# Moving the preparation of seven inputs of gated attention into the MLP, with a tile buffer of their own and a copy in DRAM

## What is computed

```
x = x + attention(layernorm(x)) @ w_ao + b_ao
x = x + attention(q from layernorm(x), k and v from ctx) @ w_co + b_co
x = x + gelu(layernorm(x) @ w1 + b1) @ w2 + b2
a = layernorm(ctx, ln_gamma, ln_beta)              # the second layer; a depends on inputs alone
Q, K, V = x @ Wq.T, a @ Wk.T, a @ Wv.T
x = x + tanh(gate) * (softmax(Q K.T / sqrt(32), masked) @ V) @ Wo.T
```

## Time and profile before

| what | value |
|---|---|
| median of 3 executions | 1102.28 us (1100.7 to 1104.54) |
| the profiled execution, its span | 1100.7 us |
| PE busy, PE weight loads busy | 1074.7 us (98%), 934.2 us (85%) |
| DVE, ACT, POOL busy | 815.4 us (74%), 712.7 us (65%), 462.0 us (42%) |
| granted TensorE clock | 1.00 throughout (2.4 GHz) |

### The profile page before, as it was taken

One profiled execution on the slowest core, in us unless ns is written; L12 is line 12 of the kernel. 1 busy time (PEld: TensorE's weight loads), 2 busy tenths in 40 slices (PEclk: granted clock), 3 DMA queues, 4 the chain that ended last, 5 costly groups with the idle time before them and its releaser, 6 DMA issues.

```text
span 1100.7 us, 24328 instructions
## 1 busy us (share of the span) xinstructions
PE 1074.7 (98%) x8829; PEld 934.2 (85%) x8829; DVE 815.4 (74%) x1314; ACT 712.7 (65%) x2365; POOL 462.0 (42%) x337
## 2 busy tenths in 40 slices
PE   7989999999999999998999999999999999999998
PEld 6888888888888888886898888888888988888886
DVE  6678787778888778888877557656677478778777
ACT  4678777777788778786444434434444387777776
POOL 3665666557767776767512121103012331122100
PEclk9999999999999999999999999999999999999999
DMA  6366565576776777553241130220622146666633
GB/s 216 98 201 198 191 195 188 174 227 216 221 227 215 223 211 229 180 191 128 85 134 40 38 96 12 85 96 1 181 101 83 59 146 205 203 198 210 177 97 97
DMA packets 136135, 167.04 MB, mean 152 GB/s; under 512 B 16992, under 2 KB 82256, under 8 KB 136016
## 3 DMA queue, kind: packets, MB, share of 16 engines
q1 hardware_dynamic: 136016, 165.50, 47.9%
HBM read 113.15 MB, written 52.29 MB: 150 GB/s over the span
## 4 chain that ended last, share of the span: by engine, by line
PE 59%; DVE 12%; ACT 9%; POOL 7%; issue 4%; DMA 3%; SPq 1%; DVEq 0%; ACTq 0%; POOLq 0%
PE psum L938 15%; PE psum L919 14%; PE psum L758 13%; POOL prob L2023 6%; PE psum L858 5%; PE psum L750 5%; ACT prob L1217 4%; ACT prob_blocks L1217 2%; PE psum L794 2%; PE psum L776 2%; DVE prob L1590 2%; DVE ln_tile L1528 2%; PE psum L835 2%; DVE negmax L1603 2%; ACT inputs_transposed L1255 2%
## 5 line engine op out<-in xcount | busy, mean ns | idle before, releaser
L758 PE MATMUL psum<-inputs_hi,weights_hi 128*128 128x256 f32 x768 | 223.7, 291 | 5.4 <-POOL inputs_lo L2014 2.5
L758 PE MATMUL psum<-inputs_lo,weights_hi 128*128 128x256 f32 x768 | 217.1, 283 | 0.0
L758 PE MATMUL psum<-inputs_hi,weights_lo 128*128 128x256 f32 x768 | 217.0, 283 | 0.0
L2014 POOL TENSOR_TENSOR inputs_lo<-inputs_transposed,inputs_hi 128x512 fp32r<-128x512 f32 x84 | 113.0, 1367 | 228.9 <-DVE inputs_hi L1563 168.4
L2023 POOL TENSOR_TENSOR prob<-prob,mask_bias 128x1024 f32<-128x1024 f32 x64 | 152.7, 2408 | 98.3 <-DVE prob L1590 96.3
L1217 ACT ACTIVATE prob<-prob,negmax 128x128 f32<-128x128 f32 x472 | 182.2, 391 | 0.5 <-DVE negmax L1603 0.5
L758 PEld LDWEIGHTS psum<-inputs_hi,weights_hi 128*128 128x128 f32 x768 | 146.7, 191 | 10.3 <-issue 2.8
L1603 DVE TENSOR_REDUCE negmax<-prob 128x8 f32<-128x1024 f32 x96 | 115.9, 1210 | 50.0 <-POOL prob L2023 50.0
L758 PEld LDWEIGHTS psum<-inputs_lo,weights_hi 128*128 128x128 f32 x768 | 147.0, 191 | 0.2
L758 PEld LDWEIGHTS psum<-inputs_hi,weights_lo 128*128 128x128 f32 x768 | 146.9, 191 | 0.0
L858 PE MATMUL psum<-weights_hi,context_parts 128*128 128x512 f32 x376 | 125.8, 393 | 0.4 <-ACT kT L1168 0.3
(11 more groups left out here) (124 smaller groups left out, 2600.3 us busy)
## 6 DMA issues: line engine op xcount, KB each, us to landing
prob_turned<-prob_blocks SPq DMA_DIRECT2D x37, 512.0 KB, 3.0
prob<-prob_turned SPq DMA_DIRECT2D x148, 128.0 KB, 3.3
weights_whole<-weights_in SPq DMA_DIRECT2D x72, 256.0 KB, 3.4
normalised<-ln_tile SPq DMA_DIRECT2D x30, 512.0 KB, 2.8
inputs_transposed<-normalised SPq DMA_DIRECT2D x120, 128.0 KB, 2.9
context<-row_sums_spread SPq DMA_DIRECT2D x188, 64.0 KB, 2.1
stream<-residual SPq DMA_DIRECT2D x42, 256.0 KB, 2.7
residual<-stream SPq DMA_DIRECT2D x42, 256.0 KB, 3.7
```

The source lines that it names most:

```text
L758: mm = pe.matmul(ps[:, bank, GT * part:GT * part + GT], w[:, slot, c, o], a[:, buf, c, :], start=c == 0 and i == 0, stop=c == KC - 1 and i ...
L2014: pool.tensor_tensor(lo, y, hi.bitcast(f32), ALU.subtract).then_inc(s_rlo if fill.ln is None else s_flo, 1)
```

## The change

Of the eight layer norm fills of D, the first (q = 0) stays as it was. The other seven are now **prepared ahead**, up to the scaled inputs, in the MLP, and these are kept in a DRAM tensor `inputs_kept`; in D each is read back with one DMA (`kind` KEPT) and only split. Fill q = 7 takes the place that q = 1 had in stretch 7. Fills q = 1 to 6 are the *second* fill of stretches 1 to 6 (`SECOND_OF_MLP`). They have tiles of their own (`ahead_tiles`): statistics in jp 6, normalising in jp 7, turning in jp 2 and scaling in jp 3 of the next stretch, and after this the store to DRAM (`keep_scaled`). They share the two buffers `inputs_transposed` with the others. What D no longer does: tile loads, statistics, inverse deviation, normalising, store, the four-DMA load, turning and scaling of these fills.

```diff
@@ planning
+HERE, AHEAD, KEPT = 0, 1, 2
+Fill = namedtuple("Fill", "ln phase q buf n kind")
 def ln_fill(ln, q, buf):
-    return Fill(ln, (A, B, None, D)[ln], q, buf, 8 * ln + q)
+    return Fill(ln, (A, B, None, D)[ln], q, buf, 8 * ln + q, KEPT if ln == 3 and q else HERE)
+def ahead_fill(q):
+    return Fill(3, None, q, None, 24 + q, AHEAD)
...
-         + [mlp_fill(q) for q in range(1, NG)] + [ln_fill(3, 0, 1), raw_fill(D, 0, 0), ln_fill(3, 1, 1)]
+         + [mlp_fill(1), mlp_fill(2)] + [f for q in range(3, NG) for f in (mlp_fill(q), ahead_fill(q - 2))]
+         + [ln_fill(3, 0, 1), raw_fill(D, 0, 0), ahead_fill(6), ahead_fill(7), ln_fill(3, 1, 1)]
...
-FILLS_OF_MLP += [[ln_fill(3, 0, 1)], [ln_fill(3, 1, 1)], [ln_fill(3, 2, 1)]]
+FILLS_OF_MLP += [[ln_fill(3, 0, 1)], [ahead_fill(7)]]
+SECOND_OF_MLP = {g: ahead_fill(g) for g in range(1, 7)}
...
+        ahead_tiles = sb("ahead_tiles", [128, 2, H])
+        kept = nc.dram_tensor("inputs_kept", (NG - 1, 128, KC * GT), f32, kind="Internal").ap()
@@ SP, load_transposed
+                elif was.kind == AHEAD:
+                    sp.wait_ge(s_keep[was.q % 2], 16 * ((was.q + 1) // 2))
...
+                if fill.kind == KEPT:
+                    sp.wait_ge(s_keep[fill.q % 2], 16 * ((fill.q + 1) // 2))
+                    sp.dma_start(transposed(fill).rearrange("p c n -> p (c n)"), kept[fill.q - 1]).then_inc(s_xt[TILE_OF[fill]], 16)
+                    return
@@ SP, keep_scaled
+            def keep_scaled(fill):
+                sp.wait_ge(s_y, PREPARED[fill] + 1)
+                sp.dma_start(kept[fill.q - 1], transposed(fill).rearrange("p c n -> p (c n)")).then_inc(s_keep[fill.q % 2], 16)
@@ SP, the MLP's loop
+                    if jp == 0 and n - 1 in SECOND_OF_MLP:
+                        store_normalised(SECOND_OF_MLP[n - 1])
+                    if jp == 1 and n - 1 in SECOND_OF_MLP:
+                        load_transposed(SECOND_OF_MLP[n - 1])
+                    if jp == 1 and n in SECOND_OF_MLP:
+                        load_tiles(SECOND_OF_MLP[n])
...
+                    if jp == 4 and n - 1 in SECOND_OF_MLP:
+                        keep_scaled(SECOND_OF_MLP[n - 1])
...
+                    if jp == 6 and n == 7:
+                        keep_scaled(ahead_fill(7))
+                        load_transposed(ln_fill(3, 1, 1))
@@ ACT, the MLP's loop, and D
+                if jp == 3 and g - 1 in SECOND_OF_MLP:
+                    fill_scale(SECOND_OF_MLP[g - 1])
...
-                fill_scale(STEPS[D][1].fill)
@@ DVE, the MLP's loop, and D
+                if jp == 2 and g - 1 in SECOND_OF_MLP:
+                    turn_inputs(SECOND_OF_MLP[g - 1])
...
+                if jp == 6 and g in SECOND_OF_MLP:
+                    statistics(SECOND_OF_MLP[g])
+                if jp == 7 and g in SECOND_OF_MLP:
+                    normalise(SECOND_OF_MLP[g])
...
-                    turn_inputs(st.fill)
...
-            statistics(ln_fill(3, 2, 1))
@@ POOL
+                if jp == 6 and g in SECOND_OF_MLP:
+                    inverse_deviation(SECOND_OF_MLP[g])
...
-            inverse_deviation(ln_fill(3, 2, 1))
```

More of the change, by code:

```diff
@@ L222, in next_fill @@
 def next_fill(fill):
-    order = [f for fills in FILLS_OF_MLP for f in fills]
-    return order[order.index(fill) + 1]
+    order = same_tiles(fill)
+    return order[order.index(fill) + 1] if fill != order[-1] else None
 def accumulator(group, t):
@@ L317, in build @@
         s_rsp = sem("row_sums_spread")
+        s_keep = [sem(f"scaled_inputs{k}_kept") for k in range(2)]
         s_pst = sem("prob_blocks_stored")
@@ L1331, in step @@
                         split(chunk)
-                if st.fill and st.fill not in TURNED:
+                if st.fill and st.fill.ln is None and st.fill not in TURNED:
                     fill_hi(st.fill)
```

73 lines of the change are left out of this document (44 added, 29 removed).

## The result

The changed kernel takes **1105.95 us** (median of 17 runs, 1103.18 to 1106.99) against 1102.28 us of the kernel before (17 runs, 1098.48 to 1104.87): ratio 1.003, 95% interval 1.002 to 1.0041 (all intervals below are of this kind). It is slower by 0.3%, 3.7 us, where 1101.2 us was forecast, and it lies above the range. The profiled execution has a span of 1105.2 us against 1100.7.

What follows compares the result with a forecast made beforehand. PE was taken as the bound, idle only around one 1.56 us stop in D, where a DMA'd mask row came late. D -1.4 and MLP +0.3 gave -1.1 us, 1102.28 to 1101.2 us; range 1098.8 to 1105.4 us.

Steps and rivals of the forecast that it cites:

- Part 3, product 14: MLP, stretch 1: added statistics use up the 1.62 us margin before w2; 0.2 us of stop, ends 0 and 1.5.
- Parts 1 and 2: D: earlier mask row of item 34 ends PE's stop, -1.4 us; other work saved lies beside busy PE, 0.
- Part 1: D, item 34: without 512 KB of loads ahead, the mask row lands sooner and PE's stop goes; -1.4 us.
- Products 27 and 28: MLP's tightest place, 0.08 us margin: added scaling delays the gelu chain; 0.1 us with stretches 5 and 7, ends 0 and 2.
- turning, normalising and SP: MLP: turning and normalising fall into DVE's waits, SP's store delays D's first weight chunks by some 6 us; 0.
- The second, slower: MLP: gelu chain breaks its margins at product 14 and in stretches 3, 5 and 7; 1107.5 us, chance 0.08.
- The first: D: mask row is late anyway, so D gives 0 and the MLP costs 0.3; 1102.6 us, chance 0.14.
- The third: D: PE isn't at its rate, so relieved engines bring pairs of items 1 us closer; 1096.2 us, chance 0.10.

Runs made afterwards that it cites:

- experiment 1: Changed kernel with stretch 1's added statistics (DVE) and inverse deviation (POOL) put behind the MLP's own fill; 1101.82 us against 1103.86 for the kernel before, ratio 0.9987.
- experiment 4: Changed kernel with only POOL's inverse deviation of stretch 1 put behind the split, statistics left ahead; 1101.63 us against 1102.34 for the kernel before, ratio 0.9991.
- experiment 8: Changed kernel with two unused 256 KB loads put back ahead of the row-sum spreading in item 33; 1104.22 us (one run) against 1103.86 for the kernel before.
- experiment 9: Kernel before with step 33's two tile loads cut from 128 rows to 16, leaving out input; 1100.8 us against 1102.34, ratio 0.9985.
- experiment 6: Changed kernel with cast and split of the MLP's own stretch 1 fill moved to product 14's head; 1102.54 us against 1102.37 for the kernel before, ratio 0.9999.
- experiment 2: Kernel before with three unused 128x512 POOL additions ahead of the split of the MLP's fill in stretch 1; 1109.65 us against 1103.86, ratio 1.0057.
- experiment 7: Kernel before with step 33's two tile loads issued behind the mask row of item 34 instead of ahead; 1107.32 us against 1103.86, ratio 1.0036.

## Why the prediction was wrong

**Part 3, product 14, is the step that failed.** The text says of the added statistics that "POOL's split of the MLP's own fill moves with them and stays beside the gelu". The split was looked at only as a neighbour that might slow DVE down. It also has a consumer: the first product of weight unit 16 waits for it, with 0.39 us in hand. A step that is moved or delayed has to be followed to whoever waits for it, and this one was not. The rows of it (583.65 + 3.10 against 587.14) were in the trace of before. By the rows that I had, 1.7 us of statistics less 0.39 give a stop of 1.3 us. POOL's inverse deviation, named as "two small instructions each" and costed at nothing, takes 1.6 us (583.78 to 585.38 in experiment 1), and ahead of the split it makes 2.9. Measured, in traces in which the turning of the fill didn't wait for its DMA: 0.9 us of stop with the statistics alone in front (experiment 4) and 2.5 us with both (experiment 8); the changed kernel's own profile has 3.5 us, with a DMA that was 0.9 us late on top.

**What I costed there instead was nearly right and didn't matter.** The gelu's low part of product 14 ends in the changed kernel at 586.20 + 1.75 = 587.95 us, and without the stop w2 would have been due at 585.35 + 0.23 + 2.72 = 588.30 us: 0.23 us is the step of one matmul, and 2.72 us the length of the product of unit 16 in the kernel before, from 587.14 to 589.86 us. So 0.35 us of the margin of 1.62 were left, with POOL's late split beside this very instruction; in experiment 1, where the split comes first, it ends at 586.03 us and w2 starts at 587.52, 1.5 us later. The 0.2 us of stop I took, and the end of 1.5, did not come.

**The clock was not in the sum at all.** No term, end or rival priced a stop at more than its length. Of the 6.5 us that the MLP lost in the profiled execution, 2.8 are of this kind. With the stop found and priced at its length my sum would have been -1.4 + 2.9 = +1.5 us instead of -1.1, so 1103.8 us, inside the range and still 2.2 under what was measured.

**The range isn't what its own terms give.** From 1100.7 and 1104.4 us, with a median that can fall 1.5 us either way, it would be 1099.2 to 1105.9 us, not 1098.8 to 1105.4. The measured 1105.95 lies just above that too, and its cause is in none of the terms.

**Parts 1 and 2 were right, Part 1 for a reason that holds only partly.** D gave 1.55 us against -1.4, and 0 after item 33 (181.12 against 181.15 us). The mask row landed 2.9 us after its issue, sooner than the 3.1 taken, and DVE waited 0.41 us for it where I had said it would not; the reciprocal still came in time:

```profile
900.46 0.23 DVE L1632 TENSOR_SCALAR mask_bias<-mask_rows 128x128 f32<-128x128 uint8 x1 [0.41 <-DMA mask_rows<-mask_d_in]
```

That the loads ahead of it were the cause is shown for the kernel before (experiment 9) and not for any program (experiment 8).

**Products 27 and 28 held**, and the other places of stretches 3, 5 and 7 with them: PE has no other wait from 555 to 850 us than the one of 3.5 us. The low part of product 28 ends at 669.78 + 0.69 = 670.47 us and its use starts at 670.83, 0.36 us of margin where the earlier trace rows had 0.08:

```profile
669.78 0.69 DVE L1738 SCALAR_TENSOR_TENSOR hidden_parts<-kT,hidden_parts 128x512 fp32r<-128x512 f32 x1
...
670.83 0.39 PE L986 MATMUL psum<-weights_hi,hidden_parts 128*128 128x512 f32 x1
```

The 0.1 us for them was not needed, nor was anything for turning, normalising and SP.

**The rivals.** The second, slower, had the sign and the engine chain, but the wrong place: the gelu chain didn't break anywhere in the changed kernel. What it describes did happen in experiment 6, where a split beside product 13 broke it. The first didn't happen. The third didn't either: pairs of items are as far apart as before, 29.08 us, with 18.4 us less work on DVE from 905 to 1046 us, so the 16 us without a weight load, which the prediction names as room, gave nothing back.

## What to carry to other kernels

Ask of every instruction that an edit pushes back, also of the untouched ones behind it on the same engine and on the next, who waits for it and how many tenths of a us are in hand; idle time of an engine says nothing on that. If work is put into a gap, put it behind what is due next, on every engine of its chain: here moving one statement on POOL and one on DVE was worth 4 us. Before a transfer is moved behind another, look at which of the two its consumer takes first.

## What the hardware showed that I had not expected

- **A stop of PE can cost nearly twice its length, and its length alone doesn't say whether it will.** With the stops of 2.9, 3.5 and 4.8 us in stretch 1 the granted clock was 1.2 GHz for 3.4 or 6.8 us; with those of 0.9 to 1.7 us, and with the one of 2.5 us, it was 2.4 GHz throughout. Elsewhere in the traces stops of much the same length went both ways: at the row sums of item 31 one of 2.33 us in the kernel before had nothing behind it, and one of 2.30 us in experiment 9 was followed by 3.4 us at half clock, as was one of 1.97 us at 372 us in experiment 2. What decides is open.
- **The same small DMA landed at different speed in the two programs.** The mask row of item 34, 16 KB behind the same four spreading DMAs, landed in 2.9 to 3.1 us in the seven traces of the changed kernel and its variants, and in 3.5 to 4.6 us in the four of the kernel before with its full loads, ahead of the row or, in experiment 7, behind it. Other mask rows of the changed program are not always that fast (2.8 to 4.4 us over the 16 of experiment 4), so the difference belongs to this place.
- **POOL's add of 128x512 took 1.41 us where I had reckoned 1**, and its split took 3.10 us beside the gelu's L1670 and L1678 in the kernel before, and 2.65 us in experiment 1, where BATCH_NORM_STATS2 runs beside its first half. The statistics, 1.28 us a pair there and in the changed kernel without a split beside them, were not slowed by it, while L1726 and L1734 in experiment 6 were, by 1.1 and 1.0 us.
